# A six-layer local-attention kernel on one core: another order of work in a slot, LN half read in place, one 64x64 tile, logits in pairs

## What is computed

```python
x = attn_layer(shift_tokens(x), Wqkv, q_scale, k_scale, Wo) + x
x = ffn_layer(shift_tokens(x), ln_g, ln_b, W1, b1, W2, b2) + x
# shift_tokens: the second half of the features comes from the token before
# attn_layer: qkv = x @ Wqkv (16 heads of 64); q, k l2-normed, scaled, rotated;
#   window of 32: a block of 32 queries sees its own 32 keys and the 32 before;
#   softmax; out @ Wo
# ffn_layer: layer norm, a * gelu(gate) with 341 inner features, @ W2 + b2
```

## Time and profile before

| | us |
|---|---|
| median of 3 runs | 2065.31 |
| lowest, highest | 2059.34, 2075.24 |
| the profiled execution | 2061.48 |
| its span | 2059.7 |

### The profile page before, as it was taken

The page is one execution under the profiler, slowest core; times in us unless marked ns, Lnnn a source line. Parts: engine busy times, 40 slices in busy tenths (PEclk is TensorE's granted clock), DMA queues, the critical chain, the costliest instruction groups (busy, mean ns, idle before and its releaser), DMA issues.

```text
span 2059.7 us, 86637 instructions
## 1 busy us (share of the span) xinstructions
PE 1797.2 (87%) x33584; PEld 1401.8 (68%) x33584; DVE 1600.0 (78%) x3772; ACT 1384.6 (67%) x3701; POOL 1332.1 (65%) x1226
## 2 busy tenths in 40 slices
PE   6999878998879898789988899988898988899887
PEld 3445457777667776677776677776677776677766
DVE  5766679898468987488896589885689885689984
ACT  3677657777557776567775577775577775577765
POOL 3444467777467777377775477774677773677773
PEclk9999979999989999999999999999899999899999
DMA  5000021111021111111110211110211110211111
GB/s 121 4 5 5 1 70 33 35 37 32 25 64 41 31 36 28 63 34 33 40 31 23 68 40 31 41 31 23 64 44 31 31 42 22 65 37 37 31 33 46
DMA packets 59120, 77.81 MB, mean 38 GB/s; under 512 B 16608, under 2 KB 31674, under 8 KB 57914
## 3 DMA queue, kind: packets, MB, share of 16 engines
q1 hardware_dynamic: 58938, 75.36, 13.9%
HBM read 22.63 MB, written 1.05 MB: 11 GB/s over the span
## 4 chain that ended last, share of the span: by engine, by line
PE 60%; DVE 15%; issue 12%; ACT 6%; POOL 5%; SPq 0%; DMA 0%; DVEq 0%; ACTq 0%; POOLq 0%
PE proj_ps L455 7%; PE s_ps L476 7%; PE tr_ps L465 7%; PE y_ps L524 7%; PE proj_ps L457 5%; PE proj_ps L456 5%; PE y_ps L516 4%; DVE by_cos L1091 3%; PE pv_ps L506 3%; ACT square L816 3%; DVE by_sin L1091 3%; DVE xs L1352 3%; PE s_ps L571 3%; DVE sumsq L1103 2%; PE s_ps L691 2%
## 5 line engine op out<-in xcount | busy, mean ns | idle before, releaser
L1502 POOL TENSOR_TENSOR qk<-by_cos,by_sin 128x512 f32<-128x512 f32 x388 | 495.3, 1276 | 208.3 <-DVE by_sin L1091 201.9
L1509 POOL TENSOR_TENSOR qk<-qk,inv_norm 128x512 f32<-128x512 f32 x388 | 404.8, 1045 | 68.7 <-ACT inv_norm L822 41.6
L1091 DVE TENSOR_TENSOR by_cos<-proj_ps,tab 128x512 f32<-128x512 f32 x364 | 249.4, 685 | 159.6 <-ACT square L816 158.6
L816 ACT ACTIVATE square<-proj_ps 128x512 f32<-128x512 f32 x364 | 217.4, 597 | 195.1 <-PE proj_ps L457 194.8
L1515 POOL TENSOR_TENSOR s_sb<-s_sb,row_max 128x512 f32<-128x512 f32 x192 | 202.7, 1056 | 136.1 <-DVE row_max L1122 136.1
L455 PE MATMUL proj_ps<-w_hi,x_hi 128*128 128x512 f32 x546 | 273.8, 502 | 4.8 <-DVE by_sin L1091 2.6
L465 PE MATMUL tr_ps<-ident,qk 128*128 128x128 f32 x1544 | 247.2, 284 | 24.2 <-ACT x_hi L810 11.8
L1103 DVE TENSOR_REDUCE sumsq<-square 128x8 f32<-128x512 f32 x388 | 262.2, 676 | 0.0
L1091 DVE TENSOR_TENSOR by_sin<-proj_ps,tab 128x512 f32<-128x512 f32 x364 | 247.8, 681 | 0.0
L465 PEld LDWEIGHTS tr_ps<-ident,qk 128*128 128x128 f32 x1544 | 184.0, 146 | 72.5 <-POOL qk L1509 28.5
L457 PE MATMUL proj_ps<-w_hi,x_lo 128*128 128x512 f32 x546 | 222.1, 407 | 0.0
(11 more groups left out here) (172 smaller groups left out, 4167.1 us busy)
## 6 DMA issues: line engine op xcount, KB each, us to landing
arena<-v SPq DMA_DIRECT2D x388, 130.0 KB, 2.4
w_raw<-in_L_ffn_Wqkv SPq DMA_DIRECT2D x7, 1536.0 KB, 7.3
wo<-in_L_ffn_Wo SPq DMA_DIRECT2D x7, 512.0 KB, 3.8
w_raw<-in_L_ffn_W SPq DMA_DIRECT2D x7, 341.0 KB, 5.5
c_in<-in_ctx SPq DMA_DIRECT2D x16, 64.0 KB, 1.8
xn<-in_fside_BxS SPq DMA_DIRECT2D x1, 1024.0 KB, 6.0
out<-z SPq DMA_DIRECT2D x4, 256.0 KB, 3.0
w<-in_L_ffn_W SPq DMA_DIRECT2D x12, 64.0 KB
```

The costliest lines, as they stand in the source:

```text
L1091: return dve.tensor_tensor(dst[:, c % 2, :].rearrange("p (h d) -> p h d", d=DH), ps, tb, ALU.mult)
L1502: pool.tensor_tensor(heads(qk[:, c, :]), heads(by_cos[:, c % 2, :]), heads(by_sin[:, c % 2, :])[:, :, ::-1, :], ALU.add).then_inc(qk_added, 1)
L1509: pool.tensor_tensor(ap, ap, inv_norm[:, c, :].unsqueeze(2).to_broadcast([128, 8, DH]), ALU.mult).then_inc(qk_ready, 1)
```

## The change

- The order of a slot is written anew on PE, ACT, DVE and POOL. On DVE the helper `step` goes, and the calls stand one by one.
- `xs` and `stats` change: only the half from `y_ps` is copied (now the first thing in `ln_stats`); the first half is read in `z`. There are two `bn_stats` and two `tensor_scalar` for `xn`, one a half.
- `QUERIES` replaces the loop over four blocks of queries: the first two are one tile of 64 rows x 64 columns, the other two stay 64x32.
- `x_scores` does a pair of groups: bias of g, logits of g, logits of g+1, bias of g+1.

```diff
+QUERIES = [(slice(0, 2 * WINDOW), 1), (slice(2 * WINDOW, 3 * WINDOW), 2), (slice(3 * WINDOW, 4 * WINDOW), 3)]
-        xs = sb("xs", [128, 2, D])
+        xs = sb("xs", [128, 2, D // 2])
-        stats = sb("stats", [128, 2, 6])
+        stats = sb("stats", [128, 2, 2, 6])
 ...
# scores, and in the same way values
-                        for w in range(NT // WINDOW):
-                            feat, toks = slice(64 * r, 64 * r + 64), slice(WINDOW * w, WINDOW * w + WINDOW)
+                        for toks, w in QUERIES:
+                            feat = slice(64 * r, 64 * r + 64)
 ...
# PE, x-stage
+            def x_bias(T, par, g, first):
+                hi, lo = flat(pos_hi[:, GH * g:GH * g + GH]), pos_lo[g]
+                pe.matmul(s_ps[:, g % 2, :], d_hi[:, par], hi, start=first, stop=False)
+                pe.matmul(s_ps[:, g % 2, :], d_hi[:, par], lo, start=False, stop=False)
+                return pe.matmul(s_ps[:, g % 2, :], d_lo[:, par], hi, start=False, stop=not first)
+            def x_logits(T, par, g, first):
+                rows = slice(32 * g, 32 * g + 32)
+                return pe.matmul(s_ps[:, g % 2, :], xq[rows, par, :], flat(xk_bd[rows, par]), start=first, stop=not first)
             def x_scores(T, par, g):
                 if g == 0:
                     pe.wait_ge(d_split, T + 1)
                 if not after(T, 1):
-                    pe.wait_ge(diag_ready, g + 1)
+                    pe.wait_ge(diag_ready, g + 2)
                 if after(T, 1) or g >= 2:
                     pe.wait_ge(masked, T * 4 + (g - 1))
 ...
+                x_bias(T, par, g, True)
                 if g == 0:
                     pe.wait_ge(xk_ready, T + 1)
+                if after(T, 1) or g >= 2:
+                    pe.wait_ge(masked, T * 4 + g)
+                x_logits(T, par, g, False).then_inc(s_full, 1)
+                x_logits(T, par, g + 1, True)
+                x_bias(T, par, g + 1, False).then_inc(s_full, 1)
 ...
# PE, slot: the order after
+                    scores(T, par, 0)
+                        project(T + 1, 0)
+                        p_transpose(T - 1, 1)
+                        project(T + 1, 1)
+                    qk_transpose(T, 3)
+                        shift_state(T - 2, tile_of(z, n - 2, D // 2))
+                        values(T - 1, 1 - par, 1)
+                        project(T + 1, 2)
+                        att_transpose(T - 1, 0)
+                    scores(T, par, 1)
+                        project(T + 1, 3)
+                        qk_transpose(T + 1, 0)
+                        att_transpose(T - 1, 1)
+                    p_transpose(T, 0)
+                        project(T + 1, 4)
+                        qk_transpose(T + 1, 1)
+                        project(T + 1, 5)
+                    values(T, par, 0)
+                        x_transpose(T + 2)
+                        out_project(T - 1, L)
 ...
# ACT, slot: the order after
+                        norms(T, 3)
+                        square_chunk(T + 1, 0)
+                        p_out(T - 1, 1)
+                        square_chunk(T + 1, 1)
+                    qk_out(T, par, 3)
+                        norms(T + 1, 0)
+                        att_out(T - 1, 0)
+                        v_out(T + 1, 1 - par, 0)
+                    exps(T, 0)
+                        square_chunk(T + 1, 2)
+                        norms(T + 1, 1)
+                        qk_out(T + 1, 1 - par, 0)
+                        att_out(T - 1, 1)
+                        ln_std(T - 2, par)
+                    p_out(T, 0)
+                        qk_out(T + 1, 1 - par, 1)
+                        square_chunk(T + 1, 3)
+                        norms(T + 1, 2)
+                        x_out(T + 2)
+                        v_out(T + 1, 1 - par, 1)
+                    exps(T, 1)
+                        qk_out(T + 1, 1 - par, 2)
 ...
# DVE
                 def ln_stats(T, n, par):
-                    zt = tile_of(z, n, 0, D // 2)
                     dve.wait_ge(sh_full, T + 1)
-                    dve.tensor_scalar(xs[:, par, 0:D // 2], zt, 1.0, None, ALU.mult).then_inc(xs_ready, 1)
-                    dve.tensor_copy(xs[:, par, D // 2:D], y_ps[:, 0:D // 2]).then_inc(xs_ready, 1)
-                    dve.wait_ge(xs_ready, T * 2 + 2)
-                    dve.bn_stats(stats[:, par], xs[:, par]).then_inc(stat_done, 1)
+                    dve.tensor_copy(xs[:, par], y_ps[:, 0:D // 2]).then_inc(xs_ready, 1)
+                    dve.bn_stats(stats[:, par, 0], tile_of(z, n, 0, D // 2))
+                    dve.wait_ge(xs_ready, T + 1)
+                    dve.bn_stats(stats[:, par, 1], xs[:, par]).then_inc(stat_done, 1)
 ...
                 def ln_apply(T, n, par):
+                    for lo, src in ((0, tile_of(z, n, 0, D // 2)), (D // 2, xs[:, par])):
+                        last = dve.tensor_scalar(tile_of(xn, n, lo, lo + D // 2), src,
+                                                 mean_var[:, par, 0:1], rstd[:, par:par + 1], ALU.subtract, ALU.mult)
+                    last.then_inc(xn_ready, 1)
# DVE, slot: the order after
+                        add_out(T - 2, n - 2)
+                    mask(T, 0)
+                    row_maxima(T, 0)
+                        times_cos(T + 1, 0, L - 1)
+                        sum_squares(T + 1, 0)
+                        times_sin(T + 1, 0, L - 1)
+                        clamp_norm(T + 1, 0)
+                        ln_stats(T - 2, n - 2, par)
+                        times_cos(T + 1, 1, L - 1)
+                        times_sin(T + 1, 1, L - 1)
+                        sum_squares(T + 1, 1)
+                        sums_inverse(T - 1, 1)
+                        normalise(T - 1, 1)
+                        ln_variance(T - 2, par)
+                        clamp_norm(T + 1, 1)
+                    mask(T, 1)
+                        times_cos(T + 1, 2, L - 1)
+                        times_sin(T + 1, 2, L - 1)
+                    row_maxima(T, 1)
+                        sum_squares(T + 1, 2)
+                        stage(T + 2, n + 2, L * 4 + 12)
+                        clamp_norm(T + 1, 2)
+                        ln_apply(T - 2, n - 2, par)
+                        times_cos(T + 1, 3, L - 1)
+                        sum_squares(T + 1, 3)
+                        times_sin(T + 1, 3, L - 1)
+                        clamp_norm(T + 1, 3)
+                    sums_inverse(T, 0)
+                    normalise(T, 0)
 ...
# POOL, slot: the order after
+                        scale_rotated(T, 3)
+                    center(T, 0)
+                        add_rotated(T + 1, 0)
+                        scale_rotated(T + 1, 0)
+                        add_rotated(T + 1, 1)
+                        scale_rotated(T + 1, 1)
+                        add_rotated(T + 1, 2)
+                    center(T, 1)
+                        scale_rotated(T + 1, 2)
+                        split_x(T + 2)
+                        add_rotated(T + 1, 3)
```

More of the change, by code:

```diff
@@ L501, in values @@
                     for r in range(2):
-                        for w in range(NT // WINDOW):
-                            i, toks = slot_of(r, w), slice(WINDOW * w, WINDOW * w + WINDOW)
+                        for toks, w in QUERIES:
+                            i = slot_of(r, w)
                             keys = slice(64 * i, 64 * i + 64)
@@ L599, in x_slot @@
                     x_values(T - 1, 1 - par, 1)
-                x_scores(T, par, 1)
-                if not first:
                     x_p_transpose(T - 1, 3)
@@ L705, in slot @@
                         p_transpose(T - 1, 1)
-                    if behind >= 2:
-                        shift_state(T - 2, tile_of(z, n - 2, D // 2))
+                    if front_on:
+                        project(T + 1, 1)
                     if first:
@@ L710, in slot @@
                     qk_transpose(T, 3)
-                    if front_on:
-                        project(T + 1, 1)
+                    if behind >= 2:
+                        shift_state(T - 2, tile_of(z, n - 2, D // 2))
                     if behind >= 1:
                         values(T - 1, 1 - par, 1)
-                        att_transpose(T - 1, 0)
                     if front_on:
                         project(T + 1, 2)
-                        qk_transpose(T + 1, 0)
+                    if behind >= 1:
+                        att_transpose(T - 1, 0)
                     scores(T, par, 1)
+                    if not front_on:
+                        f_transpose(0, tr_ps)
                     if front_on:
                         project(T + 1, 3)
-                    else:
-                        f_transpose(0, tr_ps)
-                    p_transpose(T, 0)
+                        qk_transpose(T + 1, 0)
                     if behind >= 1:
                         att_transpose(T - 1, 1)
+                    p_transpose(T, 0)
                     if front_on:
@@ L731, in slot @@
```

(69 more changed lines are left out.)

63 lines of the change are left out of this document (13 added, 50 removed).

## The result

The changed kernel takes 3481.52 us (median of 4 runs, 3464.2 to 3489.22), against 2064.48 us for the kernel before in its 4 runs beside it: 1.6841 times as long, with a 95% interval of 1.6748 to 1.6934. The forecast was 1974 us. The page of the profiled execution says which engine the time lies on.

The account below looks back on a forecast made before the run. PE and DVE were both near their limit, with PE waiting for `xs`. Gains of 74 + 5 + 14 - 2 = 91 us off 2061.5, plus 3.8 to the median, gave 1974 us; own range 1920 to 2015, 8-in-10 range 1885 to 2056.

Parts of the forecast that it names:

- the price of a change of shape inside a call: In scores and values calls, switching between 64x64 and 64x32 on separate strips: taken as nothing, with 0.20 us the other end.
- Rival 1: In scores and values calls, the array drains at every 64x64/64x32 change, 15 x 0.20 us a call: 3071 us; chance 0.15.
- The tile's gain: PE's scores and values calls: fewer matmuls save 0.15 us each, four calls a slot, taking PE from 13.98 to 13.4 us.
- The order of a slot: Layer slots: 13.4 us floors on PE and DVE plus 1.05 of waiting make 14.45 us, a gain of 0.95.
- the wait for `xs`: PE's `att_transpose` (L516) waits for DVE's L1353, 78 times, 102.7 us in all; 1.34 us in the slot read, should go.
- waits for POOL: DVE's three `tensor_scalar` a slot (`z_stage`, two halves of `xn`) wait for POOL instructions under way: 1.05 us a slot.
- LN half in place: DVE's LN input: dropping L1352 saves 0.68 us, added `bn_stats` and `xn` halves cost 0.2 each; DVE falls to 13.4 us.
- the mechanism that the prediction described for L1352: On DVE, an SBUF-to-SBUF `tensor_scalar` waits for the POOL instruction under way: 0.14 us at best, 0.76 in the median.
- Rival 2: In slots, two of DVE's three `tensor_scalar` catch a fresh 1.05 us POOL instruction: 15.5 us a slot, 2053 us; chance 0.12.
- Logits in pairs: Cross-attention x-slots: pairing two groups' logits shortens 16 slots by 0.85 us, 14 us, less 2 us at the start.
- Rival 3: In slots, the tile edit gives nothing, PE stays at 14.0 us with 0.65 of new waits: 1995 us; chance 0.15.
- rival 4: In slots, the order fits and both PE and DVE reach their floor, 13.5 us: 1876 us; chance 0.12.

Follow-up runs that it names:

- the version with four tiles: The changed kernel with four 64x32 tiles in each call, its other edits kept; 1958.17 us, 0.9478 of the kernel before.
- the grouped kernel: The changed kernel with all 64x64 tiles of a call first, then all 64x32 ones, one shape change inside; 2075.87 us, ratio 1.0055.

## Why the prediction was wrong

**The step that failed** is the price of a change of shape inside a call: "in the new calls no strip is ever used in two shapes. I take nothing, and the other end is the first rival." The runs put 0.25 us on each stretch of one shape: 3.9 us a call in place of 0.64. The argument behind the zero came from rows that show something else. Bunches of eight 64x32 tiles (two of their starts are in the earlier trace rows; the trace has eight records between 654.42 and 654.45) show that tiles of one shape on separate strips run beside each other; the step carried that over to two shapes. What the trace did have on two shapes was the other end, 0.20 us in each place that the step names. Those rows were nearest, and the forecast set them aside on a reason that no row supported. The Trainium skill's rule (TensorEngine Tiling (Array Packing), section Tiling Modes), that a change of tiling mode and not just of tile drains the engine, holds for two shapes with the same 64 rows as well: the trace now agrees, with 0.24 us a stretch. What should have weighed was the leverage: the prediction worked out that 60 changes a slot decide from 0.016 us each, a twelfth of the price of all changes seen, and still gave that case 0.15.

**Rival 1** had the mechanism, and 3071 us. Its terms: 15 changes at 0.20 us, a call of 3.8 us; measured 3.9. From the version with four tiles the drains at full clock come to 384 calls x 3.11 us = 1194 us, 1958 + 1194 = 3152 us. About 330 us of 3482 are left for the clock, which no rival had (somewhat more if part of the drains fills the 3% of a slot in which PE idled): the granted clock is at half level for 1060 us of the span, against 0.032 x 2 x 1958.9 = 125 us with four tiles, and there the same call takes 6.03 us and a projection pass 0.43 instead of 0.23. The kernel with the tile in one of the two calls shows that this comes along: 776 us over 1958 for 192 calls, 4.04 each, where the drains alone give 3.11. That PE is busy all the time does not keep the clock up here: in the 27.13 us from 1040.87 on it is busy for all of them, at a granted clock of 0.69. With half as many stretches in a call, and PE busy 97.69 of 100 us, it is 0.97. The 330 us are a difference, no experiment took the clock alone away, and why the clock falls is open.

**The tile's gain**, 0.15 us a call: nothing was there to gain. By the grouped kernel a call with the 64x64 tile costs 1.19 us with a single change inside, and 0.96 without that change's 0.23, against 0.79. The step took 0.48 us as the bound by the tiles. It overlooked that the shapes do not run beside each other, so that half of the columns stand unused at any time.

**The order of a slot** was right in its sum: 14.45 forecast, 14.40 measured, of the 102.7 us of the wait for `xs` at most 1.8 left (in the kernel with the order alone), waits for POOL 0.9 us for 1.05. Its terms were less so, and the close agreement is in part luck: the order alone, with the old copies and no saving of DVE's work, has the same slot of 14.40. PE's work stays at 14.0 us without a gain of the tile, so both engines are at 97%, PE by its work and DVE by 13.0 of its own plus 0.9 of waiting; DVE's own work came out 0.4 under the forecast's, and about 0.45 us of the slot, in which DVE idles, was not in the sum. The steady slots got shorter in every layer, from 15.35 us in the mean of neighbours to 14.40, so the gain fits all 96 slots better than 78: 96 x 0.95 = 91 us, beside the 98 us that the order alone brought. The forecast counted 79.

**LN half in place** was taken as a saving of 0.3 us of DVE's work, with 0.2 us for the added half of `xn`, which takes 0.30 when it is free. Under the new order it is worth nothing (1958.81 and 1955.83); under the old one it costs 43 us, for the larger part through the mechanism that the prediction described for L1352, in an instruction that the change adds. Rival 2, that DVE waits whole instructions of POOL, is refuted for the order as it stands (1958, not 2053), but moving `by_sin` by 0.6 us is enough to bring a part of it back: 1990.71.

**Logits in pairs**: 14 less 2 us forecast, 11 measured alone and 0.0046 in the ratio (9.5 us, from two kernels with intervals of 0.002 each) on top of the new order. The logits of a pair take 1.06 us for the 1.05 of the forecast. Rival 3, the tile without effect and PE at 14.0, had its condition right without the drains, and 1995 for a measured 1958; rival 4 (1876) asked for a floor that PE, at 14.0 us of work, could not reach. The forecast's own range of 1920 to 2015 was tighter than the bounds it names: with all of them at their ends its sum gives about 1901 and 2044.

So with the drains left out the forecast of 1974 is 16 us, 0.8%, over what the other three edits give together, part of it by errors that cancel. The mistake that made the loss was one term, and its price was left to a chance of 0.15 where the rows nearest to it said 0.2 us.

## What to carry to other kernels

Keep tiles that follow each other closely in one shape. Here a merged tile that saves a quarter of the instructions cost a quarter of a microsecond at each border with the other shape, and grouped to avoid that, it left strips unused. When an edit repeats an unknown event sixty times in a loop, multiply the nearest price in the trace by sixty first, and ask for a row, not a reason, before setting it to zero. After a reordering that leaves DVE close to full beside a busy POOL (here 97% and 82%), look at the durations of the short `tensor_scalar`s: a median far over the lowest says which of them may meet a POOL instruction, and a swap of two neighbours can move that by 0.8 us a slot.

## What the runs showed of the hardware

- A stretch of one tile shape between stretches of another costs 0.244 to 0.254 us at full clock, with two to eight passes in it, in `scores` and `values` alike. The next shape's weight load begins 0.15 us after the last matmul of the old shape started (1013.23 to 1013.38). Going from 8 to 16 stretches costs 0.234 us for each change.
- With 16 stretches a call the granted clock was at the half level for 1060 of 3462 us, with PE busy for 96% of the span, and in the slot shown for all of it. With 8 stretches it was 0.965 over the run, with 2 it was 0.976, and with equal tiles 0.968, though PE there is busy only 96.97 of 100 us of slots.
- A `tensor_scalar` of 0.30 us that starts together with a POOL instruction of 1.05 us lasts 1.10. Of two in a row, the first waiting in both kernels (0.97 in the median), the second took 0.303 us in the median where POOL's next instruction began 0.26 us or more behind its start, and 1.086 where that began within 0.1 us of it. The Trainium skill (GPSIMD Engine Reference, section Specifications) states that the SBUF interfaces are shared with VectorE, with contention for some kinds of its instructions; these rows agree that POOL can hold DVE up, and add that the wait lasts to the end of POOL's instruction.
